# Attention with L1 distances on one core: where the key terms are added, and the order of three small VectorE instructions

## Chip, core and metric

The kernel runs on one core of a Trainium2 chip. The time is device microseconds of one execution. Before the change it is 8382.76 us, the median of 3 runs (8380.82 to 8383.2).

The engines are called as in the profile: PE is TensorE, with PEld for its weight loads, DVE is VectorE, ACT is ScalarE, SP is SyncE.

## What is computed

A tokenizer, an attention block and a feed-forward block with experts, for 8 batches of 750 tokens with 64 channels, in float32. The change touches the attention alone:

```python
scale = 1.0 / sqrt(q.shape[-1])                       # width 64
a = -sum(abs(q[:, s] - k[:, t]), axis=-1) * scale     # for every query s and key t, 8 heads
a = concatenate([a, zeros((b, 1, t, h))], axis=1)     # one more logit, zero
a = softmax(a, axis=1)[:, :t]                         # over the queries
bf = einsum('bsdh,bshw->bdhw', a, vf)
bb = einsum('bdsh,bshw->bdhw', a, vb)
```

The kernel uses |q - k| / 2 = max(q, k) - (q + k) / 2. The maxima are made on DVE, the absolute values on ACT, and what belongs to q alone or k alone is added apart: per query in the bank `kept`, per key in `kx`. The softmax is exp, divided by one plus its sum.

## The kernel before

`build` runs three phases: `phase_tokens`, `phase_attend`, `phase_feed`. `phase_attend` takes from about 300 to 8120 us of the span.

**Tiling.** It works through NPAIR = 16 pairs (8 batches, two groups g of four heads), in a hardware loop over the batches with both groups written out. A pair has NT = 24 tiles. The 128 partitions of a tile are 4 heads x 32 keys, its columns are the 750 queries, in two halves of 375. A tile has eight quads of keys (the last tile of a pair has four) and every quad two parts of 32 channels. The first quad has both parts merged into one row, so a full tile has 15 rows and the last one 7; a pair has STEPS = 352 rows.

**Rows and the ring.** A row is 128 x 3000 numbers in one of RING = 6 slots. Nearly half of the single rows (positions 1, 3, 5, 8, 10, 12, 14 of a tile) are made by ACT with Abs (L919), the others (2, 4, 6, 7, 9, 11, 13) by DVE with max and add (L1013). The merged row at position 0 is DVE's: four small instructions (L953) and a long one (L956), in `both`. PE sums each row over channels into the bank `sc` of the tile (L867, 16 matmuls of 375 columns a row). Each row waits for its slot (`ring_free`, counted up by PE), and PE for each row (`made_vec`, `made_act`).

**Order by hand.** Each engine's order is written out: constants at L759 say behind which row of a tile the other work of the tile before or after stands, and where a tile is shorter, behind its last row. Positions are those of the row list, and DVE itself makes no row at 8 and 10.

- EXP_AT = 6: ACT's `finish` takes exp of the finished bank of the tile before into `ex` (L903) and sums it into `zsum`; it counts up `ex_made`.
- FILL_AT = 8: DVE's `fill` (L943) sets the bank of the tile to come to `kept` plus the key term of that tile, one number a partition, `kx[:, g, t:t+1]`. It counts up `bank_set`, for which PE waits at the tile's start. In the last tile of a pair `key_sums` (L936) stands ahead of it, which takes the next pair's key terms out of PSUM, times -0.5.
- Z_AT = 8, RZ_AT = 9, A_AT = 10: DVE's `add_one` (L962), `invert` (L967) and `scale` (L972): one plus the sum, its inverse, and `ex` times the inverse. Each waits for the one before through a semaphore (`z_made`, `rz_made`, `a_made`). They stand in the order fill, plus one, row 9, inverse, scale, row 11.
- EXT_AT = 12: DVE's `turn` transposes the scaled tile (L985).
- On PE `back` (L815) behind row 2 and `forward` behind row 5 (L829) multiply the scaled tile with the values. `forward` is left out in every sixth tile; else it has 32 matmuls (the first of five) or 40.
- `sums` on PE (L841, L845), at the start of a pair's last tile, makes the query and key sums of the next pair in `kept`.

SP loads the next pair; no load is touched by the change.

Of the kernel before, what the change touches and what calls it, by code (L numbers as in the profile page):

```python
# [6 lines left out]
ALU = mybir.AluOpType  # L7
ACT = mybir.ActivationFunctionType
# [5 lines left out]
HALF = L // 2  # L14
# [54 lines left out]
def merged(t):  # L69

    return True
# [13 lines left out]
def first_step(t):  # L85

    return sum(len(steps(u)) for u in range(t))
# [635 lines left out]
def phase_attend(nc, sbuf, psum, semaphore, at, oacc, window, ratio, select, scratch_x, scratch_qk, scratch_ks, scratch_v):  # L723

    with ExitStack() as ctx:
# [30 lines left out]
        NV = STEPS - NA  # L756
        NM = sum(merged(t) for t in range(NT))
        KX = 400
        EXP_AT, FILL_AT, Z_AT, RZ_AT, A_AT, EXT_AT, KEEP_AT = 6, 8, 8, 9, 10, 12, 14  # L759
        BACK_AT, FORWARD_AT = 2, 5  # L760

        def rows(t):
# [7 lines left out]
        def due(place, i, t):  # L770

            return i == min(place, rows(t) - 1)
# [5 lines left out]
        with nc.Block() as block:  # L778
# [27 lines left out]
            def _(pe):  # L806
# [44 lines left out]
                def tile(n, g, t, b):  # L851

                    T = n * NT + t
                    bank = sc[t % 2]
                    pe.wait_ge(bank_set, T + 1)
                    if t == NT - 1:
                        pe.wait_ge(bank_set, (n + 1) * NT)
                        sums(1 - g, b + g)
                    for i, (quad, part) in enumerate(steps(t)):
                        if scalar_step(quad, part):  # L860
                            pe.wait_ge(made_act, n * NA + made_before(t, i + 1, True))
                        else:
                            pe.wait_ge(made_vec, n * NV + made_before(t, i + 1, False))
                        slot = (first_step(t) + i) % RING
                        for h in range(2):
                            for j in range(HALF_NH):
                                mm = pe.matmul(bank[32 * j:32 * j + 32, h, 0:HALF],  # L867
                                               window[:, min(part, 1), HALF_NH * g + j, QUADS - 1 - quad:QUADS + 31 - quad],
                                               ring[:, slot, j, h * HALF:(h + 1) * HALF],
                                               start=False, stop=(i == rows(t) - 1), skip_group_check=True)  # L870
                        mm.then_inc(ring_free, 1 if t < NT - 1 or i < rows(t) - 1 else 1 + TURN - STEPS)
                        if i == BACK_AT:
                            if t >= 2:
                                back(T - 2, g, t - 2, b)
                            else:
                                back(T - 2, 1 - g, NT - 2 + t, b)
                        if i == FORWARD_AT and t % GROUP:
                            if t >= GROUP:
                                forward(n * NT + (t // GROUP * GROUP - 1), g, t // GROUP - 1, t % GROUP - 1, GROUP - 1)
                            else:  # L880
                                forward(n * NT - 1, 1 - g, NG - 1, t % GROUP - 1, GROUP - 1)
# [15 lines left out]
            @block.scalar  # L897
            def _(act):

                def finish(par, done):  # L900

                    act.wait_ge(ring_free, done)
                    act.activation(ex[par][:, :].rearrange("p (h c) -> p h c", h=2)[:, :, 0:HALF], sc[par][:, :, 0:HALF],  # L903
                                   ACT.Exp, scale=-2.0 / D ** 0.5,
                                   accum_out=zsum[:, par:par + 1]).then_inc(ex_made, 1)

                def pair(b, g):

                    n = b * 2 + g
                    act.wait_ge(pair_in[g], b * (16 * NLOADS) + 16 * NLOADS)  # L910
                    act.mul(xs[g][:, 1, :, :], xs[g][:, 0, :, :], -0.5).then_inc(halves_made, 1)
                    act.wait_ge(halves_made, n + 1)
                    for t in range(NT):
                        for i, (quad, part) in enumerate(steps(t)):
                            k = first_step(t) + i
                            c = QUADS * t + quad
                            if scalar_step(quad, part):
                                act.wait_ge(ring_free, n * TURN + (k + 1))
                                act.activation(flat(ring[:, k % RING, :, :]), flat(qx[g][:, part, :, :]), ACT.Abs,  # L919
                                               bias=xs[g][:, 1, part, c:c + 1], scale=0.5).then_inc(made_act, 1)  # L920
                            if due(EXP_AT, i, t):
                                finish((t + 1) % 2, n * TURN + (first_step(t) + RING))

                with act.Fori(0, B) as b:
                    pair(b, 0)
                    pair(b, 1)
                act.wait_ge(ring_free, NPAIR * TURN + RING)
                finish((NT - 1) % 2, NPAIR * TURN + RING)

            @block.vector  # L930
            def _(vec):

                def key_sums(pairs, g):

                    vec.wait_ge(sums_made, pairs)
                    vec.tensor_scalar(kx[:, g, :], kept[:, 0, KX:KX + NT], -0.5, None, ALU.mult).then_inc(kx_made, 1)  # L936

                def fill(pairs, g, t):

                    par = t % 2  # L940
                    vec.wait_ge(kx_made, pairs)
                    if merged(t):
                        vec.tensor_scalar(sc[par][:, :, 0:HALF], kept[:, :, 0:HALF], kx[:, g, t:t + 1], None,  # L943
                                          ALU.add).then_inc(bank_set, 1)
                    else:
                        vec.tensor_copy(sc[par][:, :, 0:HALF], kept[:, :, 0:HALF]).then_inc(bank_set, 1)

                def both(n, g, t):

# [9 lines left out]
                def add_one(T, par):  # L959

                    vec.wait_ge(ex_made, T + 3)
                    vec.tensor_scalar(rz[:, par:par + 1], zsum[:, par:par + 1], 1.0, None, ALU.add).then_inc(z_made, 1)  # L962
# [34 lines left out]
                def pair(b, g):  # L997

                    n = b * 2 + g
                    vec.wait_ge(pair_in[g], b * (16 * NLOADS) + 16 * NLOADS)  # L1000
                    vec.wait_ge(halves_made, n + 1)
                    for t in range(NT):
                        T = n * NT + (t - 1)
                        par = (t + 1) % 2
                        for i, (quad, part) in enumerate(steps(t)):
                            k = first_step(t) + i
                            c = QUADS * t + quad
                            if not scalar_step(quad, part):
                                vec.wait_ge(ring_free, n * TURN + (k + 1))
                            if part == 2:  # L1010
                                both(n, g, t)
                            elif not scalar_step(quad, part):
                                vec.tensor_scalar(flat(ring[:, k % RING, :, :]), flat(qx[g][:, part, :, :]),  # L1013
                                                  xs[g][:, 0, part, c:c + 1], xs[g][:, 1, part, c:c + 1],
                                                  ALU.max, ALU.add).then_inc(made_vec, 1)
                            if due(FILL_AT, i, t):
                                vec.wait_ge(ex_made, n * NT + (t + 2))
                                if t == NT - 1:
                                    key_sums(n + 2, 1 - g)
                                    fill(n + 2, 1 - g, 0)  # L1020
                                else:
                                    fill(n + 1, g, t + 1)
                            if due(Z_AT, i, t):
                                add_one(T, par)
                            if due(RZ_AT, i, t):
                                invert(T, par)
                            if due(A_AT, i, t):
                                scale(T, par)
                            if due(EXT_AT, i, t):
                                if t:  # L1030
                                    turn(T, n, g, t - 1)
                                else:
                                    turn(T, n, 1 - g, NT - 1)
                            if t == GROUP and due(KEEP_AT, i, t):
                                keep(n, 1 - g, b + g)

                key_sums(1, 0)
                fill(1, 0, 0)
                with vec.Fori(0, B) as b:
                    pair(b, 0)  # L1040
                    pair(b, 1)
# [553 lines left out]
```

## Time and profile before

| | |
|---|---|
| median of 3 runs | 8382.76 us |
| the profiled execution | 8385.55 us |
| its span, first to last instruction | 8383.8 us |
| mean granted clock of PE | 0.989 |
| busy over the whole span | PE 8146.3 us (97%), DVE 7988.7 (95%), ACT 7685.1 (92%) |
| rows with Abs (L919) | 2624 of 2789 ns |
| matmuls of the rows (L867) | 90112, busy 7329.8 us |
| rows with max and add (L1013) | 2624 of 1832 ns |
| fill (L943) | 385 of 1002 ns |
| exp (L903) | 385 of 772 ns, and 189 ns each for reading the sum |

A view of the waits gives the time in total, how often, and the longest. A timeline row gives start, length, engine, line, operation and tiles; consecutive like instructions are merged into one row with their count, and brackets tell idle time before it and what ended it. Lengths of neighbours may overlap a little, so what an instruction costs its engine is read from start to start.

### The profile page before, as it was taken

What the parts mean: (1) busy time and instruction counts of PE and PEld (TensorE: products, weight loads), DVE (VectorE), ACT (ScalarE), POOL (GpSimd) and SP (SyncE); (2) the same over time, 40 slices, a digit from 0 to 9 for tenths busy, and PEclk for the clock granted to TensorE, in tenths of its full rate; (3) what the DMA queues carried; (4) which work ended last, traced back from release to release, by engine and by line L of the source; (5) the groups of instructions that cost most, each with busy time, mean ns of one, the idle gap of its engine ahead of it and who ended that gap; (6) DMA issues with size and microseconds to landing.
All of it is one profiled execution on the core that took longest, in us unless ns stands there. A gap on an engine that the chain in (4) does not pass through costs nothing. (4 is left out here: it accounts for less than half of the span.)

```text
span 8383.8 us, 244371 instructions
## 1 busy us (share of the span) xinstructions
PE 8146.3 (97%) x108456; PEld 3446.9 (41%) x108456; DVE 7988.7 (95%) x6906; ACT 7685.1 (92%) x3712; POOL 39.7 (0%) x36
## 2 busy tenths in 40 slices
PE   8699999999999999999999999999999999999999
PEld 3244444444444444444444444444444444444443
DVE  4699999999999999999999999999999999999984
ACT  3599999999999999999999999999999999999986
POOL 1000000000000000000000000000000000000000
PEclk9899999999999999999999999999999999999999
DMA  4310101001010100101010010101001010100000
GB/s 130 102 25 2 25 2 25 2 2 25 2 25 2 25 2 2 25 2 25 2 25 2 2 25 2 25 2 25 2 3 24 2 25 2 25 2 2 2 20 8
DMA packets 150392, 142.53 MB, mean 17 GB/s; under 512 B 115384, under 2 KB 121528, under 8 KB 148776
## 3 DMA queue, kind: packets, MB, share of 16 engines
q1 hardware_dynamic: 135711, 105.19, 5.4%
q10 hardware_dynamic: 13584, 21.06, 0.9%
q8 instruction: 891, 14.60, 0.7%
q14 instruction: 206, 1.69, 0.1%
HBM read 84.15 MB, written 42.05 MB: 15 GB/s over the span
## 5 line engine op out<-in xcount | busy, mean ns | idle before, releaser
L919 ACT ACTIVATE ring<-qx,xs 128x3000 f32<-128x3000 f32 x2624 | 7168.6, 2789 | 358.1 <-PE sc L867 357.5
L867 PE MATMUL sc<-ring,window 128*32 128x375 f32 x90112 | 7329.8, 479 | 118.9 <-DVE ring L956 114.8
L1013 DVE TENSOR_SCALAR ring<-qx,xs 128x3000 f32<-128x3000 f32 x2624 | 4711.7, 1832 | 1.5 <-PE sc L867 1.3
L867 PEld LDWEIGHTS sc<-ring,window 128*32 128x32 f32 x90112 | 2895.8, 109 | 4278.9 <-issue 3709.6
L956 DVE SCALAR_TENSOR_TENSOR ring<-qx,xs,ring 128x3000 f32<-128x3000 f32 x384 | 1284.1, 3344 | 13.5
L953 DVE TENSOR_SCALAR ring<-qx,xs,ratio 128x750 f32<-128x750 f32 x1536 | 925.5, 668 | 21.1 <-issue 15.7
L943 DVE TENSOR_SCALAR sc<-kept,kx 128x750 f32<-128x750 f32 x385 | 385.8, 1002 | 0.6
L985 DVE STREAM_TRANSPOSE exts<-ex 128x768 f32<-128x768 f32 x385 | 374.5, 973 | 0.6
L829 PEld LDWEIGHTS acc<-exts,vf 128*32 128x32 f32 x12480 | 283.0, 109 | 119.9 <-issue 118.7
L815 PE MATMUL acc<-ex,vb 128*32 128x376 f32 x3088 | 314.3, 478 | 1.5 <-DVE ex L972 1.5
L829 PE MATMUL acc<-exts,vf 128*32 128x96 f32 (+1 forms) x12480 | 310.6, 244 | 0.2 <-DVE exts L985 0.2
L903 ACT ACTIVATE ex<-sc 128x750 f32<-128x750 f32 x385 | 297.3, 772 | 6.7 <-PE sc L867 6.7
L972 DVE TENSOR_SCALAR ex<-ex,rz 128x768 f32<-128x768 f32 x385 | 239.1, 621 | 13.7
L815 PEld LDWEIGHTS acc<-ex,vb 128*32 128x32 f32 x3088 | 99.8, 108 | 145.0 <-issue 142.9
L1477 DVE SCALAR_TENSOR_TENSOR part<-pd,b2c,cb 128x500 f32<-128x500 f32 x48 | 35.5, 739 | 110.0 <-PE pd L1260 99.6
L641 ACT ACTIVATE qx<-pq,bqw,wkr 128x750 f32<-128x750 f32 x32 | 31.2, 975 | 117.8 <-issue 59.3
L1343 ACT ACTIVATE hid<-pu,b1c 128x1000 f32<-128x1000 f32 x96 | 99.8, 1088 | 39.9 <-PE pu L1240 39.8
L1240 PE MATMUL pu<-xt_d,w1t 64*128 64x500 f32 x384 | 96.7, 623 | 0.0
L710 DVE TENSOR_TENSOR exts<-pv,bv 120x1024 f32<-120x1024 f32 x34 | 40.2, 1220 | 54.2 <-PE pv L552 53.4
L1260 PE MATMUL pd<-hid,w2t 128*64 128x500 f32 x384 | 91.1, 595 | 0.6 <-DVE part L1477 0.6
L541 PE MATMUL pq<-oacc,w 64*128 64x375 f32 x128 | 32.1, 578 | 55.7 <-ACT qx L641 54.8
L552 PE MATMUL pv<-w,oacc 64*120 64x512 f32 x200 | 60.6, 727 | 13.6 <-DVE qx L710 13.6
(170 smaller groups left out, 915.8 us busy)
## 6 DMA issues: line engine op xcount, KB each, us to landing
qx<-scratch_qk SPq DMA_DIRECT2D x240, 187.5 KB
scratch_v<-exts SPq DMA_DIRECT2D x17, 960.0 KB, 7.8
scratch_qk<-qx ACTq DMA_DIRECT2D x32, 375.0 KB, 6.3
vb<-scratch_v SPq DMA_DIRECT2D x240, 46.0 KB
vf<-scratch_v SPq DMA_DIRECT2D x120, 88.0 KB
scratch_v<-qx SPq DMA_DIRECT2D x4, 960.0 KB, 6.6
scratch_v<-qx ACTq DMA_DIRECT2D x4, 960.0 KB, 8.9
qx<-scratch_qk ACTq DMA_DIRECT2D x16, 187.5 KB
```

The costliest lines, as they stand in the source:

```text
L815: pe.matmul(acc[g][32 * u:32 * u + 32, 0:COLS], vb[g][:, t, w0:w0 + 32], ex[t % 2][:, h * HPAD:h * HPAD + COLS], start=(t == 0), stop=Fals ...
L829: mm = pe.matmul(acc[g][32 * u:32 * u + 32, 0:COLS].rearrange("p (a c) -> p a c", a=2)[:, :, lo:lo + cols], vf[g][:, k, w0:w0 + 32], buf[: ...
L867: mm = pe.matmul(bank[32 * j:32 * j + 32, h, 0:HALF], window[:, min(part, 1), HALF_NH * g + j, QUADS - 1 - quad:QUADS + 31 - quad], ring[: ...
L903: act.activation(ex[par][:, :].rearrange("p (h c) -> p h c", h=2)[:, :, 0:HALF], sc[par][:, :, 0:HALF], ACT.Exp, scale=-2.0 / D ** 0.5, ac ...
L919: act.activation(flat(ring[:, k % RING, :, :]), flat(qx[g][:, part, :, :]), ACT.Abs, bias=xs[g][:, 1, part, c:c + 1], scale=0.5).then_inc( ...
L943: vec.tensor_scalar(sc[par][:, :, 0:HALF], kept[:, :, 0:HALF], kx[:, g, t:t + 1], None, ALU.add).then_inc(bank_set, 1)
L953: vec.tensor_scalar(ring[:, slot, j, :], qx[g][:, 0, j, :], xs[g][:, 0, 0, c:c + 1], ratio[:, HALF_NH * g + j:HALF_NH * g + j + 1], ALU.ma ...
L956: vec.scalar_tensor_tensor(flat(ring[:, slot, :, :]), flat(qx[g][:, 1, :, :]), xs[g][:, 0, 1, c:c + 1], flat(ring[:, slot, :, :]), ALU.max ...
L972: vec.tensor_scalar(ex[par][:, :], ex[par][:, :], rz[:, par:par + 1], None, ALU.mult).then_inc(a_made, 1)
L985: vec.transpose(ext[(NG * g + t // GROUP) % 2][:, :, :, t % GROUP, :], ex[t % 2][:, :]).then_inc(ext_made, 1)
L1013: vec.tensor_scalar(flat(ring[:, k % RING, :, :]), flat(qx[g][:, part, :, :]), xs[g][:, 0, part, c:c + 1], xs[g][:, 1, part, c:c + 1], ALU ...
L1343: act.activation(hid[n % 2][:, u, :, :], pu[u][:, :, 0:EC], ACT.Relu, bias=b1c[:, 2 * e + u:2 * e + u + 1]).then_inc(relu_made, 1)
```

## The change

- Key terms are no longer added when the bank is filled. `fill` copies `kept` alone, and `finish` gives the key term to exp as its bias, from `kx[:, g, t:t+1]` of the tile that it finishes. As exp is taken of -0.25 times the bank, `key_sums` scales by 1/8 instead of -0.5.
- In the first tile of a pair ACT waits for `kx_made` ahead of exp, PE waits for it ahead of `sums`, `fill` waits for `sums_made` instead of `kx_made`, and a memset of `kx[:, 1, :]` stands once ahead of all.
- `add_one` stands ahead of `fill` instead of behind it, and `invert` right behind `fill` (RZ_AT 8 instead of 9), with row 9 between it and `scale`.

```diff
-        EXP_AT, FILL_AT, Z_AT, RZ_AT, A_AT, EXT_AT, KEEP_AT = 6, 8, 8, 9, 10, 12, 14
+        EXP_AT, FILL_AT, Z_AT, RZ_AT, A_AT, EXT_AT, KEEP_AT = 6, 8, 8, 8, 10, 12, 14
...
                     if t == NT - 1:
                         pe.wait_ge(bank_set, (n + 1) * NT)
+                        pe.wait_ge(kx_made, n + 2)
                         sums(1 - g, b + g)
...
-                def finish(par, done):
-
+                def finish(g, t, done):
+
+                    par = t % 2
                     act.wait_ge(ring_free, done)
                     act.activation(ex[par][:, :].rearrange("p (h c) -> p h c", h=2)[:, :, 0:HALF], sc[par][:, :, 0:HALF],
-                                   ACT.Exp, scale=-2.0 / D ** 0.5,
+                                   ACT.Exp, scale=-2.0 / D ** 0.5, bias=kx[:, g, t:t + 1],
                                    accum_out=zsum[:, par:par + 1]).then_inc(ex_made, 1)
...
                             if due(EXP_AT, i, t):
-                                finish((t + 1) % 2, n * TURN + (first_step(t) + RING))
+                                if t == 0:
+                                    act.wait_ge(kx_made, n + 2)
+                                if t:
+                                    finish(g, t - 1, n * TURN + (first_step(t) + RING))
+                                else:
+                                    finish(1 - g, NT - 1, n * TURN + RING)
...
                     vec.wait_ge(sums_made, pairs)
-                    vec.tensor_scalar(kx[:, g, :], kept[:, 0, KX:KX + NT], -0.5, None, ALU.mult).then_inc(kx_made, 1)
-
-                def fill(pairs, g, t):
+                    vec.tensor_scalar(kx[:, g, :], kept[:, 0, KX:KX + NT], 1.0 / D ** 0.5, None, ALU.mult).then_inc(kx_made, 1)
+
+                def fill(pairs, t):
 
                     par = t % 2
-                    vec.wait_ge(kx_made, pairs)
-                    if merged(t):
-                        vec.tensor_scalar(sc[par][:, :, 0:HALF], kept[:, :, 0:HALF], kx[:, g, t:t + 1], None,
-                                          ALU.add).then_inc(bank_set, 1)
-                    else:
-                        vec.tensor_copy(sc[par][:, :, 0:HALF], kept[:, :, 0:HALF]).then_inc(bank_set, 1)
+                    vec.wait_ge(sums_made, pairs)
+                    vec.tensor_copy(sc[par][:, :, 0:HALF], kept[:, :, 0:HALF]).then_inc(bank_set, 1)
...
+                            if due(Z_AT, i, t):
+                                add_one(T, par)
                             if due(FILL_AT, i, t):
                                 vec.wait_ge(ex_made, n * NT + (t + 2))
                                 if t == NT - 1:
                                     key_sums(n + 2, 1 - g)
-                                    fill(n + 2, 1 - g, 0)
+                                    fill(n + 2, 0)
                                 else:
-                                    fill(n + 1, g, t + 1)
-                            if due(Z_AT, i, t):
-                                add_one(T, par)
+                                    fill(n + 1, t + 1)
                             if due(RZ_AT, i, t):
                                 invert(T, par)
...
+                vec.memset(kx[:, 1, :], 0.0).then_inc(kx_made, 1)
                 key_sums(1, 0)
-                fill(1, 0, 0)
+                fill(1, 0)
```

## Rows read from the trace of the kernel before

**Rows 1.** Busy time by window: us of window, PE, PEld, DVE, ACT, POOL, PEclk, DMA, GB/s.

```profile
1000.00:8000.00 7000.00, 6896.27 (x94876) 2927.42 (x94872) 6952.21 (x5821) 6678.40 (x3062) 0.00 (x0) 1.00 0.05 11
```

**Rows 2.** Waits from 1000 to 8000 us: total us, times, longest.

```profile
ACT ring L919 <- PE sc L867: 321.0, 677, 6.2
...
PE sc L867 <- DVE ring L956: 100.0, 60, 5.6
...
DVE ring L953 <- PE sc L867: 4.7, 9, 0.6
```

**Rows 3.** Timeline of DVE, two tiles from fill to fill, and the next L956.

```profile
7972.63 1.00 DVE L943 TENSOR_SCALAR sc<-kept,kx 128x750 f32<-128x750 f32 x1
7973.54 0.15 DVE L962 TENSOR_SCALAR rz<-zsum 128x1 f32<-128x1 f32 x1
7973.60 1.84 DVE L1013 TENSOR_SCALAR ring<-qx,xs 128x3000 f32<-128x3000 f32 x1
7975.35 0.16 DVE L967 RECIPROCAL rz<-rz 128x1 f32<-128x1 f32 x1
7975.55 0.62 DVE L972 TENSOR_SCALAR ex<-ex,rz 128x768 f32<-128x768 f32 x1
...
7980.45 2.41 DVE L953 TENSOR_SCALAR ring<-qx,xs,ratio 128x750 f32<-128x750 f32 x4
...
7993.16 1.00 DVE L943 TENSOR_SCALAR sc<-kept,kx 128x750 f32<-128x750 f32 x1
...
8023.95 3.34 DVE L956 SCALAR_TENSOR_TENSOR ring<-qx,xs,ring 128x3000 f32<-128x3000 f32 x1
```

**Rows 4.** Timeline of PE in the same stretch, to the end of a bare tile.

```profile
7974.00 1.01 PE L829 MATMUL acc<-exts,vf 128*32 128x96 f32 x40
7974.82 15.46 PE L867 MATMUL sc<-ring,window 128*32 128x375 f32 x192
7990.10 0.81 PE L815 MATMUL acc<-ex,vb 128*32 128x376 f32 x8
...
8011.26 15.34 PE L867 MATMUL sc<-ring,window 128*32 128x375 f32 x192
8027.35 3.05 PE L867 MATMUL sc<-ring,window 128*32 128x375 f32 x36 [0.75 <-DVE ring L956]
```

**Rows 5.** Groups of DVE instructions by form: busy us, mean ns, idle before.

```profile
L943 DVE TENSOR_SCALAR sc<-kept,kx 128x750 f32<-128x750 f32 x385 | 385.8, 1002 | 0.6
L972 DVE TENSOR_SCALAR ex<-ex,rz 128x768 f32<-128x768 f32 x385 | 239.1, 621 | 13.7
L363 DVE TENSOR_SCALAR state<-ps 128x750 f32<-128x750 f32 x24 | 22.6, 940 | 38.2 <-PE ps L296 38.2
L993 DVE COPY oacc<-acc 128x375 f32 x8 | 4.3, 544 | 0.0
```

**Rows 6.** Timeline of a pair's end, DVE and then PE.

```profile
3721.32 0.18 DVE L936 TENSOR_SCALAR kx<-kept 128x24 f32<-128x24 f32 x1
3721.54 1.01 DVE L943 TENSOR_SCALAR sc<-kept,kx 128x750 f32<-128x750 f32 x1
3722.45 0.15 DVE L962 TENSOR_SCALAR rz<-zsum 128x1 f32<-128x1 f32 x1
3722.64 0.16 DVE L967 RECIPROCAL rz<-rz 128x1 f32<-128x1 f32 x1
3722.84 0.62 DVE L972 TENSOR_SCALAR ex<-ex,rz 128x768 f32<-128x768 f32 x1
...
3730.20 4.00 PE L867 MATMUL sc<-ring,window 128*32 128x375 f32 x48 [3.08 <-DVE ring L956]
```

**Rows 7.** Groups of ACT instructions by form.

```profile
L903 ACT ACTIVATE ex<-sc 128x750 f32<-128x750 f32 x385 | 297.3, 772 | 6.7 <-PE sc L867 6.7
L1343 ACT ACTIVATE hid<-pu,b1c 128x1000 f32<-128x1000 f32 x96 | 99.8, 1088 | 39.9 <-PE pu L1240 39.8
```

**Rows 8.** The table load of ACT at L911, same view.

```profile
L911 ACT ACT_TABLE_LOAD x8 | 10.3, 1283 | 7.8 <-PEq L469 7.7
```

More of the change, by code:

```diff
@@ L927, in _ @@
                 act.wait_ge(ring_free, NPAIR * TURN + RING)
-                finish((NT - 1) % 2, NPAIR * TURN + RING)
+                finish(1, NT - 1, NPAIR * TURN + RING)
             @block.vector
```

## The prediction

> **What bounds the kernel now.** I read the views in this order: the page's busy times and slices, the busy time of the long middle window, the list of waits, then single instructions of two or three tiles on each engine, then a pair's end.
>
> The middle window holds the attention stage, at full granted clock. TensorE (PE), VectorE (DVE) and ScalarE (ACT) are all over 95% busy in it [rows 1], so shares don't name the bound and the waits have to. In the same 7000 us DVE's line L953 waited 4.7 us for PE, in nine places. PE waited 100 us for DVE's line L956, in 60 places, and ACT waited 321 us for PE [rows 2]. The chain is ACT behind PE and PE behind DVE, with DVE behind nobody: DVE's own instructions, start to start, are the period. The page's chain view doesn't help, since it covers 3% of the span, in the last stage.
>
> One tile, from fill to fill on DVE, is 7993.16 - 7972.63 = 20.53 us [rows 3]. PE does a tile's work in less. A run of matmuls has a recorded tail that overlaps the next work: 7974.82 + 15.46 - 7990.10 = 0.18 us. Twelve steps that run on without a wait are recorded as 15.34 us, less the tail 15.16 us, or 1.263 us a step; twelve around a tile's start, where PE meets line L956, take 7990.10 - 7974.82 = 15.28 us [rows 4]. So PE loses 0.12 us at the start of a tile with 40 matmuls of `forward`. A tile without `forward` (every sixth) leaves 0.75 us of recorded idle time, 0.93 us with the tail [rows 4]. A tile with 32 of them (also every sixth) is shorter than one with 40 by 8 x 0.82 / 40 = 0.16 us, and loses 0.28 us. PE's own work is therefore 20.41 us in a 40-tile, 20.25 in a 32-tile, 19.60 in a bare one. A pair has 23 full tiles: 15, 4 and 4 of these, a mean of 20.24 us. That is the floor once DVE is faster than PE: 0.29 us a tile below today.
>
> ACT is busy 95.4% of the window [rows 1], or 19.6 us of 20.53.
>
> **The change, part by part.**
>
> *Fill without a pointer operand (L943, 385 times).* It is 1002 ns for 750 columns, from PSUM to PSUM, with one operand read from a [128,1] tile [rows 5]. The nearest rows without such an operand are 940 ns for 750 columns from PSUM to SBUF (L363) and 544 ns for a COPY of 375 columns from PSUM (L993) [rows 5]. The two differ by 396 ns for 375 columns, that is 1.05 ns a column, so the copy isn't in a double-rate mode. With 1.04 ns a column the fixed parts are 221 ns (L943), 159 (L363) and 154 (L993). L972, SBUF to SBUF at half that per column, has 621 - 400 = 221 with one pointer, while L962 is 0.15 us for one column with an immediate [rows 3, 5]. Two pairs of rows thus give 62 to 70 ns for the pointer and almost nothing for PSUM against SBUF as the target. I take 65 ns. Bounds: 0 (if writing PSUM and not the pointer costs it) and 72.
>
> *The order of the three small instructions.* Now: fill, plus one, a ring row, inverse, scale. L967 starts at 7975.35 and L972, which waits for its result, at 7975.55 [rows 3]: 0.20 us for an instruction of 0.16 us; at the pair's end L962 and L967, each waited for in the same way, show 0.19 and 0.20 [rows 6]. I take 0.195. Where nothing depends on the instruction ahead, the next starts 0.09 us before that one's recorded end: L962 to L1013 is 0.06 us [rows 3]. At a pair's end, where `z_made` has to be waited for at once, the same L967 starts 0.19 us after L962 [rows 6], and between ring rows L967 starts before the row's end [rows 3]. The cost is that of the pair, not of the line. In the new order plus one stands ahead of the fill (0.85 us cover `z_made`), the inverse behind it, and a ring row (1.75 us) between inverse and scale covers `rz_made`. The inverse then costs 0.07 instead of 0.195: 0.125 us a tile. If the cover were gone it would be today's cost. Bounds 0 and 0.135.
>
> By the Trainium skill ("VectorE: DVE Perf Modes", section "The DRAIN you can't avoid") eight copies with a semaphore after each took as long as eight with one at the end, so a semaphore between neighbours would cost nothing, and this term would be nil. The rows here speak against it, with 0.195 beside 0.06 us; it is a rival below.
>
> *A full tile:* 0.065 + 0.125 = 0.19 us, all on the path, as DVE waits for nobody. 23 x 16 = 368 tiles: 69.9 us.
>
> *A pair's end (16 times).* Key terms, fill, plus one, inverse, scale stand together. From L936 to L972 it is 3722.84 - 3721.32 = 1.52 us [rows 6]. Of this 0.22 us is the step from L936 to the fill, which waits for `kx_made`. After: plus one 0.06, key terms 0.09 (0.18 less the 0.09 overlap, since the copy needs no key term), fill 0.91 - 0.065 = 0.845, inverse and its wait 0.195: 1.19 us. It saves 0.33 us, and PE sits idle 3.08 us just behind it [rows 6], so all of it counts: 5.3 us.
>
> *Exp with a bias.* It is 772 ns for 750 columns now [rows 7]; at 0.833 ns a column its fixed part is 147. L1343 (bias read from a tile) has 1088 - 833 = 255 [rows 7]. So the operand costs some 108 ns, and I add 0.11 us a tile to ACT. ACT has 0.93 us a tile free, 0.74 after the shorter period and 0.63 with the bias: nothing, and nothing either at twice the price. Its results have room: in the middle window no wait of DVE for ACT is listed, and DVE reaches the fill (and then plus one, behind the same wait) no sooner than now but for the 0.19 us. Only the very last exp stands bare: +0.1 us once.
>
> *Waits.* Plus one now waits for `ex_made` ahead of the fill, which waited for the same value before: nothing new. ACT's `kx_made` wait at a pair's first exp and PE's ahead of `sums` ask for a value set at the previous pair's end, many us earlier. Behind ACT's would stand ring rows, behind PE's a whole tile. The memset lies in DVE's wait for the first `sums`. No DMA or queue is moved.
>
> *What is late next.* DVE's new period is 20.34 us. PE in a 40-tile needs 20.41, so PE falls 0.07 behind in each of four tiles in a row, 0.28 in all, and regains it in the bare tile. DVE may only run ahead by what the ring of six slots allows. It begins the merged row (L953) at 7980.45, for which PE must have finished step 9: 7974.82 + 4 x 1.263 + tail 0.18 = 7980.05, and 0.06 for the release (as L956's end at 8027.29 to PE's start at 8027.35) [rows 3, 4]. Room is 0.34 us, 0.15 after a saving of 0.19, less the lag at the tile's start (0, 0.07, 0.14, 0.21). So DVE is held up by some 0.06 us once in six tiles: 0.06 x 3 x 16, about 3 us.
>
> **Sum.** 69.9 + 5.3 - 0.1 - 3 = 72 us. The profiled execution took 8385.55 us with a span of 8383.8, 2.8 us above the median. I carry the saving to the median: 8382.76 - 72 is 8311 us.
>
> **Rivals.**
>
> *PE takes over in the 40-tiles.* If the ring's room is really nil, lag can't be carried and 15 tiles a pair run at 20.41 instead of 20.34: 15 x 16 x 0.07 = 17 us lost of 75, 8325 us. For: the room is small, and PE's ends are modelled. Against: DVE waited for PE in so few places.
>
> *The copy costs as much as the sum.* Writing PSUM from PSUM has no row without a pointer. Then 0.125 x 368 + 0.265 x 16 = 50 us are gained, less held-up time: 8334 us.
>
> *Waiting costs nothing.* What looks like a wait would belong to the scale itself: it starts late behind whatever stands ahead. Then only the copy saves, 0.065 x 384 = 25 us: 8358 us. Against: L967 appears with both spacings [rows 3, 6]. The skill's DRAIN section, above, would give this time.
>
> *ACT becomes last (slower).* Place: exp, between ring rows 5 and 8 of ACT. If exp with its bias needs another table than the Abs rows around it, two loads a tile come in. ACT would have 19.6 + 2 x 1.28 = 22.2 us a tile: 1.6 x 384 = 620 us more, 9000 us. It decides from 0.93 us of extra work a tile. The 1.28 us is that of the loads in this trace, which has one at L911 in half of the pairs [rows 8] and none between Abs and Exp; a bias doesn't change the function, so it is unlikely.
>
> *More than forecast.* If the overlap is deeper than 0.09 us, the saving goes on until PE's floor: 0.29 x 368 + 5 = 112 us, 8271 us; half of the way from the forecast is 8291.
>
> *It does nothing.* The gaps close elsewhere on DVE (each moved instruction takes up the saving as another stall): within 0.2%.
>
> **How the numbers follow.** The forecast has 0.62; PE takes over 0.13; costly copy 0.10; waiting costs nothing 0.04; more than forecast 0.05; nothing 0.03; slower 0.03. The range goes from 8297 (with the upper bounds of both terms, 0.207 us a tile, and nothing held up, 82 us are gained, 8301, and 4 us are for scatter and for a start of the case of more) to 8336 (costly copy with 2 us of scatter). What lies outside (waiting costs nothing, most of more than forecast, nothing, slower) is some 0.15. A measurement of this kernel tells about 0.2%, 17 us, from no change: all cases but the last two are faster by more, so faster 0.94, same 0.03, slower 0.03.
>
> **What the profile will show.** Fill a COPY of 930 to 940 ns; L967's successor 0.07 us behind it and the scale without idle time ahead; 20.34 us from fill to fill; exp 870 ns, with ACT's wait for PE down by a quarter or more; PE's recorded idle time at bare tiles down from 0.75 to some 0.3; 2.4 to 2.8 us instead of 3.08 at a pair's end; a few more waits of L953 for PE. The prediction is wrong if the copy stays at 1000 ns, if the scale still stands 0.03 us or more behind its predecessor, or if L953 waits for PE in most tiles.

## The result and the profile after

The changed kernel takes 8318.88 us (median of 4 runs, 8315.86 to 8326.73), beside 8382.98 us for the kernel before (4 runs): a ratio of 0.9923, 95% interval 0.9911 to 0.9936, or 64 us less. The forecast was 72 us less, 8311 us, in a range of 8297 to 8336. A second series of the changed kernel (5 runs, below) has 8323.09 us beside 8385.2, 62 us less. The profiled execution of after took 8326.73 us, its slowest, with a span of 8324.7.

The groups of the page of after (busy us, mean ns, idle before), to be held against [rows 5, 7]; the rows of L921 and L868 are those of L919 and L867 in the table of before:

```profile
L921 ACT ACTIVATE ring<-qx,xs 128x3000 f32<-128x3000 f32 x2624 | 7162.0, 2790 | 265.3 <-PE sc L868 261.5
L868 PE MATMUL sc<-ring,window 128*32 128x375 f32 x90112 | 7311.4, 479 | 86.8 <-DVE ring L959 86.6
...
L949 DVE COPY sc<-kept 128x750 f32<-128x750 f32 x385 | 359.9, 935 | 0.0
...
L905 ACT ACTIVATE ex<-sc,kx 128x750 f32<-128x750 f32 x385 | 333.5, 866 | 6.6 <-PE sc L868 6.6
...
L975 DVE TENSOR_SCALAR ex<-ex,rz 128x768 f32<-128x768 f32 x385 | 236.0, 613 | 0.6
```

The fill is 935 ns for 1002, the exp 866 for 772, and the idle time ahead of the scale is 0.6 us in all instead of 13.7. A tile on DVE, from plus one to plus one (timeline: start, length, both us):

```profile
3602.82 0.14 DVE L965 TENSOR_SCALAR rz<-zsum 128x1 f32<-128x1 f32 x1
3602.88 0.93 DVE L949 COPY sc<-kept 128x750 f32<-128x750 f32 x1
3603.73 0.15 DVE L970 RECIPROCAL rz<-rz 128x1 f32<-128x1 f32 x1
3603.80 1.82 DVE L1016 TENSOR_SCALAR ring<-qx,xs 128x3000 f32<-128x3000 f32 x1
3605.54 0.61 DVE L975 TENSOR_SCALAR ex<-ex,rz 128x768 f32<-128x768 f32 x1
...
3623.14 0.15 DVE L965 TENSOR_SCALAR rz<-zsum 128x1 f32<-128x1 f32 x1
```

The inverse now costs 3603.80 - 3603.73 = 0.07 us from start to start, and the scale begins before the ring row ahead of it has ended (3603.80 + 1.82 = 3605.62). The tile is 20.32 us, 20.33 in most, where it was 20.53. The end of a pair, DVE and then PE, answers to [rows 6]:

```profile
3702.79 0.15 DVE L965 TENSOR_SCALAR rz<-zsum 128x1 f32<-128x1 f32 x1
3702.86 0.17 DVE L943 TENSOR_SCALAR kx<-kept 128x24 f32<-128x24 f32 x1
3702.95 0.94 DVE L949 COPY sc<-kept 128x750 f32<-128x750 f32 x1
3703.79 0.15 DVE L970 RECIPROCAL rz<-rz 128x1 f32<-128x1 f32 x1
3703.98 0.62 DVE L975 TENSOR_SCALAR ex<-ex,rz 128x768 f32<-128x768 f32 x1
...
3711.34 1.14 PE L868 MATMUL sc<-ring,window 128*32 128x375 f32 x9 [2.43 <-DVE ring L959]
```

It takes 3703.98 - 3702.79 = 1.19 us for 1.52, and PE idles 2.43 us instead of 3.08. The waits from 1000 to 8000 us, as [rows 2]:

```profile
ACT ring L921 <- PE sc L868: 236.7, 389, 6.0
...
PE sc L868 <- DVE ring L959: 74.3, 64, 5.0
...
DVE ring L956 <- PE sc L868: 11.3, 11, 2.2
...
DVE ring L1016 <- PE sc L868: 5.1, 16, 0.7
```

ACT waits a quarter less for PE and PE a quarter less for DVE, while DVE has begun to wait for PE now and then. That is where a part of the gain went. From the start of the first L956 or L959 to that of the last, the attention stage, it is 7796.5 us before and 7729.5 after: 67.0 us saved. The terms, each summed over all tiles from the starts of that line:

| | forecast, us | measured, us |
|---|---|---|
| shorter period of 368 full tiles | 69.9 | 73.6 (0.20 each) |
| ends of pairs | 5.3 | 4.7 (in 15 of 16) |
| DVE held up in the long tiles | -3 | -6 |
| first tile behind the loop's turn and the start | 0 | -4.3 |
| sum | 72 | 68 |

Rounding the period to 0.01 us is the last 1 us. The profiled executions differ by 58.8 us and not by 67.0 because attention began at 309.5 us in the trace of before and at 318.0 in that of after; in a second trace of after it began at 306.6, and the earlier phases are the same code in all. Such scatter outside the stage may also be what separates 67 us from the 64 of the medians; no trace shows it for these.

### The profile page after: what moved, and what is told of

Same layout as the page of the kernel before. It is cut to its first block and busy times, and to the rows that moved or that the text cites. A ratio compares the mean times of both kernels' runs of the same rounds, so it can differ in the third digit from the quotient of the medians.

```text
span 8324.7 us, 244412 instructions
## 1 busy us (share of the span) xinstructions
PE 8114.0 (97%) x108456; PEld 3999.8 (48%) x108456; DVE 7931.1 (95%) x6907; ACT 7711.0 (93%) x3712; POOL 39.7 (0%) x36
## 5 line engine op out<-in xcount | busy, mean ns | idle before, releaser
L921 ACT ACTIVATE ring<-qx,xs 128x3000 f32<-128x3000 f32 x2624 | 7162.0, 2790 | 265.3 <-PE sc L868 261.5
L868 PE MATMUL sc<-ring,window 128*32 128x375 f32 x90112 | 7311.4, 479 | 86.8 <-DVE ring L959 86.6
L868 PEld LDWEIGHTS sc<-ring,window 128*32 128x32 f32 x90112 | 3424.7, 110 | 3689.3 <-issue 2751.4
L1016 DVE TENSOR_SCALAR ring<-qx,xs 128x3000 f32<-128x3000 f32 x2624 | 4705.7, 1829 | 5.3 <-PE sc L868 5.1
L959 DVE SCALAR_TENSOR_TENSOR ring<-qx,xs,ring 128x3000 f32<-128x3000 f32 x384 | 1283.9, 3343 | 13.6
L956 DVE TENSOR_SCALAR ring<-qx,xs,ratio 128x750 f32<-128x750 f32 x1536 | 924.8, 665 | 22.1 <-PE sc L868 11.9
L949 DVE COPY sc<-kept 128x750 f32<-128x750 f32 x385 | 359.9, 935 | 0.0
L905 ACT ACTIVATE ex<-sc,kx 128x750 f32<-128x750 f32 x385 | 333.5, 866 | 6.6 <-PE sc L868 6.6
```

What stands on the lines that cost most here:

```text
L868: mm = pe.matmul(bank[32 * j:32 * j + 32, h, 0:HALF], window[:, min(part, 1), HALF_NH * g + j, QUADS - 1 - quad:QUADS + 31 - quad], ring[: ...
L956: vec.tensor_scalar(ring[:, slot, j, :], qx[g][:, 0, j, :], xs[g][:, 0, 0, c:c + 1], ratio[:, HALF_NH * g + j:HALF_NH * g + j + 1], ALU.ma ...
L959: vec.scalar_tensor_tensor(flat(ring[:, slot, :, :]), flat(qx[g][:, 1, :, :]), xs[g][:, 0, 1, c:c + 1], flat(ring[:, slot, :, :]), ALU.max ...
```

## Experiments

The order, copy, immediate and spread kernels ran beside 10 runs of the kernel before with a median of 8386.25 us, the bias, ring and loop-turn kernels beside 15 runs with 8384.91, the last two beside 9 with 8385.2.

**The order alone.** The kernel before, with `RZ_AT` 8 and `add_one` ahead of `fill`:

```diff
-        EXP_AT, FILL_AT, Z_AT, RZ_AT, A_AT, EXT_AT, KEEP_AT = 6, 8, 8, 9, 10, 12, 14
+        EXP_AT, FILL_AT, Z_AT, RZ_AT, A_AT, EXT_AT, KEEP_AT = 6, 8, 8, 8, 10, 12, 14
...
+                            if due(Z_AT, i, t):
+                                add_one(T, par)
                             if due(FILL_AT, i, t):
```

> The kernel before with the new order alone: plus one ahead of the fill, inverse right behind it, the key term still added in the fill. Theory (the wait for a neighbour's result costs DVE 0.125 us): from fill to fill 20.53 becomes 20.40 to 20.41 us, the idle time ahead of the scale (13.7 us in all before) is gone, and the time falls by 0.125 x 368 + 0.13 x 16 = 48 us, to 8333 to 8338. Rival (the scale starts late by itself, waiting costs nothing): scale still 0.03 us behind its predecessor's end, 20.50 us or more, less than 10 us gained. At 20.41 us DVE is as slow as PE in its longest tiles, so no tile should be held up by the ring.

Measured: 8336.34 us (4 runs), ratio 0.9942, interval 0.9927 to 0.9958, 50 us less. From the DVE timeline:

```profile
3515.75 1.00 DVE L943 TENSOR_SCALAR sc<-kept,kx 128x750 f32<-128x750 f32 x1
3516.66 0.15 DVE L967 RECIPROCAL rz<-rz 128x1 f32<-128x1 f32 x1
3516.73 1.83 DVE L1013 TENSOR_SCALAR ring<-qx,xs 128x3000 f32<-128x3000 f32 x1
3518.47 0.62 DVE L972 TENSOR_SCALAR ex<-ex,rz 128x768 f32<-128x768 f32 x1
```

The inverse costs 0.07 us, and the scale starts before the ring row ahead of it has ended (3516.73 + 1.83 = 3518.56). The period is 20.39 us in every full tile but 0 and 6 (6 has `keep`, 0.45 us more in all kernels), so the order is worth 0.14 us a tile, a little over the forecast's 0.125. The rival that waiting costs nothing is out.

**The copy alone.** The kernel after, in the old order (fill, plus one, row, inverse, scale; the reverse of the diff above):

> The kernel after with the old order: fill as a copy, then plus one, a ring row, inverse, scale; key terms as the bias of exp. Theory (the pointer operand costs 0.065 us): 20.46 us from fill to fill, 0.065 x 368 plus 16 pair ends of 0.19 us, 27 us gained, 8353 to 8358. Rival (the gain of the change is mostly in the copy, the order is worth nothing): 20.33 us, 8320. The gains of this kernel and of the one with the order alone should add up to more than that of the change, by what the ring takes back (7 us by the trace of after).

Measured: 8358.52 us (5 runs), ratio 0.9968, interval 0.9955 to 0.9981, 28 us less; the period is 20.47 us. The inverse and the scale stand 0.20 us apart again:

```profile
3512.79 0.16 DVE L970 RECIPROCAL rz<-rz 128x1 f32<-128x1 f32 x1
3512.99 0.62 DVE L975 TENSOR_SCALAR ex<-ex,rz 128x768 f32<-128x768 f32 x1
```

The two gains are 50 and 28 us, 78 together; the change itself has 62 to 64 at its medians. In the traces the attention stage is 26.2 us shorter with the copy, 47.5 with the order and 67.0 with both (68.9 in the second trace of after), so 5 to 7 us are missing in the sum, as expected; the rest of what is missing in the medians is within their scatter. The copy alone leaves DVE above the 20.41 us that PE needs in a long tile, and the order alone brings it to 20.39, where no tile is held up yet. Both together bring it 0.08 us below.

**Operand or operation.** The kernel after with

```diff
-                    vec.tensor_copy(sc[par][:, :, 0:HALF], kept[:, :, 0:HALF]).then_inc(bank_set, 1)
+                    vec.tensor_scalar(sc[par][:, :, 0:HALF], kept[:, :, 0:HALF], 0.0, None, ALU.add).then_inc(bank_set, 1)
```

> The kernel after with the fill as an addition of the immediate 0.0 instead of a copy, PSUM to PSUM as before. If the operand read from a tile cost the time, the fill takes 935 to 945 ns and a tile 20.33 to 20.34 us, 8316 to 8321 in all. If it was the addition as against a copy, it takes 1000 ns, a tile 20.39 us, and 24 us of the gain are gone (8340).

Measured: 8317.59 us (4 runs), ratio 0.9919, interval 0.9903 to 0.9934. Its group:

```profile
L949 DVE TENSOR_SCALAR sc<-kept 128x750 f32<-128x750 f32 x385 | 361.0, 938 | 0.0
```

938 ns, as the copy. What cost 64 ns in L943 is the operand that is read from a tile, not the addition and not PSUM as the target.

**Exp with a bias alone.** The kernel before, with a tile of zeros:

```diff
-                                   ACT.Exp, scale=-2.0 / D ** 0.5,
+                                   ACT.Exp, scale=-2.0 / D ** 0.5, bias=kz[:, par:par + 1],
```

> The kernel before with exp given a bias read from a tile of zeros; all else as before. Theory (ACT has 0.9 us a tile to spare): exp 865 to 870 ns instead of 772, ACT's wait for PE 30 to 40 us less, a tile still 20.53 us, the time within 4 us of before. Rival (ACT's lateness reaches PE or DVE): each tile longer by up to 0.1 us, 35 us slower.

Measured: 8384.03 us (10 runs) beside 8384.91 (15 runs), ratio 0.9999, interval 0.999 to 1.0008. The group of exp, and ACT's wait from 1000 to 8000 us:

```profile
L905 ACT ACTIVATE ex<-sc,kz 128x750 f32<-128x750 f32 x385 | 333.4, 866 | 6.6 <-PE sc L869 6.6
```

```profile
ACT ring L921 <- PE sc L869: 271.1, 472, 6.0
```

ACT is busy 31 us more in these 7000 us (6709.87 for 6678.40), which is 94 ns for each of some 336 tiles. It comes out of ACT's wait for PE, 271 us for 321, and no tile is longer (20.53). ACT pays for the operand in time it has.

**Is it the ring that takes gain back?** In after, DVE's periods are 20.33 us, tiles 0 and 6 apart, but for the tiles 10, 11, 16, 17 and 22 of a pair, with means of 20.39, 20.44, 20.38, 20.43 and 20.40. They are the last tiles with 40 matmuls of `forward` before a bare one or the pair's end. Here is tile 11 of one pair, DVE and PE, and one row of the bare tile behind it:

```profile
3588.30 1.80 DVE L1016 TENSOR_SCALAR ring<-qx,xs 128x3000 f32<-128x3000 f32 x1
3590.09 2.42 DVE L956 TENSOR_SCALAR ring<-qx,xs,ratio 128x750 f32<-128x750 f32 x4
...
3608.72 1.80 DVE L1016 TENSOR_SCALAR ring<-qx,xs 128x3000 f32<-128x3000 f32 x1
3610.43 2.41 DVE L956 TENSOR_SCALAR ring<-qx,xs,ratio 128x750 f32<-128x750 f32 x4
...
3583.96 1.02 PE L829 MATMUL acc<-exts,vf 128*32 128x96 f32 x40
3584.79 15.37 PE L868 MATMUL sc<-ring,window 128*32 128x375 f32 x192
...
3616.27 4.00 PE L868 MATMUL sc<-ring,window 128*32 128x375 f32 x48 [0.31 <-DVE ring L959]
```

PE's row 9 ends at 3584.79 + 4 x 1.263 + 0.18 = 3590.02 us, and with 0.06 for the release DVE may start at 3590.08; it starts at 3590.09, 1.79 us behind the start of the row ahead where a tile later it is 1.71. PE's idle time at the bare tile is 0.31 us for 0.75: PE was behind and caught up there. Two experiments press on this from both sides.

*Less room:* `RING = 5`.

> The kernel after with five slots in the ring instead of six. Theory (DVE begins the merged row of the next tile only when PE has finished the row six before it, with some 0.15 us to spare): with five slots it has to wait for one row more, 1.26 us. From the end of row 10 on PE, the release and the tail take 0.24 us, the merged row 2.45 + 3.26 us and its release 0.06 us, in which PE has only four rows (5.05 us) to do: it stands still 1.0 us a tile. A tile takes 21.2 us in the mean, all 8620 to 8670 us. L956 waits for PE in nearly every tile. Rival (the ring has room to spare and the small hold-ups of tiles 10, 11, 16, 17, 22 come from elsewhere): 8315 to 8330 us.

Measured: 8681.17 us in one run, beside 8384.91 us. PE and DVE timelines:

```profile
3502.36 4.00 PE L868 MATMUL sc<-ring,window 128*32 128x375 f32 x48 [0.98 <-DVE ring L959]
...
3511.25 11.56 PE L868 MATMUL sc<-ring,window 128*32 128x375 f32 x144
3523.67 4.00 PE L868 MATMUL sc<-ring,window 128*32 128x375 f32 x48 [0.85 <-DVE ring L959]
...
3517.82 2.41 DVE L956 TENSOR_SCALAR ring<-qx,xs,ratio 128x750 f32<-128x750 f32 x4 [0.60 <-PE sc L868]
```

Row 10 ends at 3511.25 + 5 x 1.263 + 0.18 = 3517.75, released 0.06 later: L956 starts at 3517.82. PE stands still 0.85 us as recorded, 1.03 with the tail. The place is as expected; the total is 11 us above the range given. Most long tiles came to 21.48 us, 32-tiles to 21.31, bare ones to 20.65, the mean of all full tiles to 21.4 us, where 21.2 was expected. L956 waits for PE 313 times between 1000 and 8000 us, in nearly every tile, but the single rows (L1016) wait too, 271 times and 99 us in all, which the expectation didn't have. This single run is far outside of what the rival gave.

*Shorter tiles:* the forward products of a pair's first two groups in six parts of 32 matmuls instead of four of 40 and one of 32, so that the tiles 7 to 18 are alike:

```diff
-                        if i == FORWARD_AT and t % GROUP:
-                            if t >= GROUP:
-                                forward(n * NT + (t // GROUP * GROUP - 1), g, t // GROUP - 1, t % GROUP - 1, GROUP - 1)
+                        if i == FORWARD_AT and t and t != GROUP:
+                            q = (t - 1) // GROUP
+                            parts = GROUP if q in (1, 2) else GROUP - 1
+                            if q:
+                                forward(n * NT + (q * GROUP - 1), g, q - 1, (t - 1) % GROUP, parts)
                             else:
-                                forward(n * NT - 1, 1 - g, NG - 1, t % GROUP - 1, GROUP - 1)
+                                forward(n * NT - 1, 1 - g, NG - 1, t - 1, parts)
```

> The kernel after with the forward products of a pair's first two groups of tiles cut into six parts (32 matmuls each) instead of five, so that tiles 7 to 18 need 20.25 us of PE each and none needs 20.41. Theory (PE's lag in its long tiles uses up the room in the ring and holds DVE up): tiles 10, 11, 16 and 17, at 20.36 to 20.46 us in the trace of after, come to 20.33; tile 22 keeps its 20.40; PE's recorded idle time in the bare tiles is gone. 0.35 x 16 = 5 to 6 us faster than after. Rival (those tiles are slow for another reason, such as a port or the clock): they keep 20.40 to 20.45, and the time stays within 2 us.

Measured: 8313.46 us (5 runs), ratio 0.9915, interval 0.9901 to 0.9928. The tiles 10, 11, 16 and 17 are at 20.33 us in the mean of all pairs, tile 22 keeps 20.38. Summed over the tiles 1 to 22, 5.3 us less than in after are above the common period. PE's timeline at a bare tile that has become a 32-tile:

```profile
3587.38 3.97 PE L868 MATMUL sc<-ring,window 128*32 128x375 f32 x48
3591.17 0.84 PE L829 MATMUL acc<-exts,vf 128*32 128x96 f32 x32
3591.83 15.44 PE L868 MATMUL sc<-ring,window 128*32 128x375 f32 x192
3607.08 0.81 PE L815 MATMUL acc<-ex,vb 128*32 128x376 f32 x8
```

From 3591.17 to the same row 20.33 us later nothing is idle by more than the 0.09 us that the twelve rows' 15.25 us have over 15.16. The comparison was repeated with both kernels side by side:

> The changed kernel once more, beside the one with six forward parts, to compare the two on one chip. 8313 to 8322 us; tiles 10, 11, 16, 17 and 22 at 20.35 to 20.45 us as in its first trace; at the loop's turns tile 0 is held up by the PE time lost to the clock less 0.5 to 1.0 us.

> Six forward parts in the first two groups of a pair, as before. Theory (ring room): 4 to 7 us less than the changed kernel beside it. Rival (the gain in the tiles is given back elsewhere): within 2 us of it.

Measured: 8323.09 us (8314.81 to 8323.8, 5 runs) for the changed kernel and 8313.62 us (8312.33 to 8320.47, 5 runs) for the other. The medians differ by 9.5 us, more than expected, but the ranges overlap: the ratios to before are 0.9925 (0.9912 to 0.9939) and 0.9916 (0.9902 to 0.9929). What the traces carry is 5 us in the held-up tiles: the tiles 1 to 22 are 5.8 us above the common period in the changed kernel and 0.7 in the other. The whole attention stage is only 2.7 us shorter in this pair of traces (7725.0 for 7727.7), since the first tiles behind the loop's turn, below, are held up by 2.7 us more; in the pair before it was 4.3 us shorter (7725.2 for 7729.5). So it is shown that the held-up tiles go back to the common period when no tile needs 20.41 us of PE. That the whole kernel is faster by it isn't clear of the noise, though both medians of this kernel are the lowest of all that were tried.

**Behind the loop's turn.** The first tile of a pair behind the turn of the hardware loop is longer in both kernels. In after, in one such place (PE timeline, then granted clock in windows, the third number from the right):

```profile
1288.61 6.71 PE L868 MATMUL sc<-ring,window 128*32 128x375 f32 x45 [4.78 <-DVE ring L959]
```

```profile
1288.00:1292.00 4.00, 3.39 (x21) 1.26 (x25) 4.00 (x3) 2.22 (x3) 0.00 (x0) 0.50 0.01 4
...
1296.00:1300.00 4.00, 4.00 (x56) 1.80 (x52) 3.63 (x6) 3.64 (x2) 0.00 (x0) 1.00 0.00 0
```

PE was idle for 4.78 us, then ran at half the full clock, the 1.2 GHz level, and 45 matmuls took 6.71 us where 48 take 4.00. It falls behind, and DVE is held up once the ring's room is used. With the PE time lost to the clock behind each of the seven turns, from windows of 1 us, and the hold-up of the tile there:

| kernel | period, us | lost to clock, seven turns, us | hold-up, us | at a loss near 3.0 | at a loss near 1.5 |
|---|---|---|---|---|---|
| before | 20.53 | 14.3 | 5.8 | 1.77 | 0.15 to 0.18 |
| copy alone | 20.47 | 12.8 | 5.7 | 1.85 | 0.26 to 0.70 |
| order alone | 20.39 | 16.0 | 9.5 | 2.22 | 0.47 |
| after | 20.33 | 17.3 | 11.8 | 2.09, 2.55 | 0.71, 0.78 |
| after, second trace | 20.33 | 14.1 | 8.7 | 2.11 | 0.58 to 0.84 |

At about the same loss the hold-up is 0.3 to 0.8 us larger after than before. The difference of the two sums, a seventh of it for each turn, is what the ring's room takes up: 1.21 us before, 1.01 with the copy, 0.93 with the order, 0.79 and 0.77 after. It shrinks with DVE's period, and 1.21 - 0.79 is 3 us in seven turns that are due to the change. The rest of the difference is that the loss itself differs from turn to turn (1.4 to 3.1 us) and from trace to trace; why it does stays open. The first tiles of the other pairs are held up by 3.0 us in all before and 1.3 after, so that the term of the table above is 4.3 us in this trace of after and 2.0 in the second. An attempt to keep PE busy there:

```diff
+                    if t == 0 and g == 0:
+                        for _ in range(36):
+                            pe.matmul(acc[1][:, 400:512], select[:, :], ksum[:, 0:112], start=True, stop=True,
+                                      skip_group_check=True)
                     pe.wait_ge(bank_set, T + 1)
```

These matmuls start sums of their own in the bank in which the sums of `acc[1]` stand. This kernel and the next don't compute the reference's output, presumably because they disturb those sums; that wasn't tested apart. The work and its order are otherwise those of after.

> The kernel after with 36 small matmuls (bf16, 112 columns, into columns of a bank that nobody reads) ahead of the first tile of every second pair, where the loop turns and PE is idle for 4.8 us; in the trace of after PE's granted clock falls to the half just there and PE's slow first rows hold DVE up for 0.7 to 2.5 us (13.1 us in all over the 20.33 us of a tile, 8.8 before the change). Theory (the idle time lets the clock fall): the clock stays at 1.00 behind the loop's turn, tile 0 takes 20.3 to 20.8 us there, 6 to 10 us are gained on after. Rival (the hold-up is of another kind, or the matmuls don't keep the clock up): tile 0 stays at 21 to 22.9 us, no gain, or up to 2 us lost where the small matmuls are in the way.

Measured: 8337.41 us (5 runs), ratio 0.9944, interval 0.993 to 0.9958, 14 to 19 us slower than after. PE's timeline and a window:

```profile
1274.98 0.26 PE L857 MATMUL acc<-ksum,select 128*128 128x112 bf16 x2 [2.35 <-issue]
1278.05 3.35 PE L857 MATMUL acc<-ksum,select 128*128 128x112 bf16 x34 [2.81 <-issue]
1281.33 5.08 PE L872 MATMUL sc<-ring,window 128*32 128x375 f32 x48
```

```profile
1276.00:1280.00 4.00, 1.95 (x22) 1.96 (x23) 4.00 (x3) 3.03 (x3) 0.00 (x0) 0.59 0.02 4
```

PE can't start them: it stands 2.35 us and, two matmuls on, 2.81 us more with no wait that the profile names. The first of these stops is in the trace of after too, at the branch that closes the loop on PE (L890; count, length in ns, start in us):

```profile
L890 PEldq COMPARE_BRANCH  x1: 3866/3866/3866, 1282.4 to 1282.4; - x1
L890 PEldq FUSED_REGOPS  x1: 63/63/63, 1286.3 to 1286.3; - x1
```

There PE is idle from 1283.83 to 1288.61 us and its branch ends at 1286.22. So 2.4 of the 4.8 us that the profile puts down to a wait for L959 are PE's own stop; for the other 2.4 PE waits for DVE, which had a stop of 2.2 us at its own branch. Whether a second stop of 2.8 us hides under that wait isn't shown. In the kernel with the small matmuls the clock has fallen by the time they run (0.59), they take 0.1 us each and the first tile is later still (23 to 25 us behind the turns), a loss well beyond the 2 us that the rival allowed. These matmuls don't hold the clock. Whether it would stay up if PE had no idle time there, and what would remove PE's stop, wasn't tried.

> The small matmuls at the loop's turn together with the forward products cut into six parts. If the two hold-ups are separate, both gains add up: 12 to 15 us on after, 8302 to 8307 us. If only the spread works, 8313 us.

Measured: 8328.19 us (5 runs), ratio 0.9933, interval 0.992 to 0.9947. That misses both figures given. As the small matmuls cost time instead of saving it, what is left is that this cost and the gain of the spread stand side by side: 9 us less than with the small matmuls alone.

## Why the prediction was right

**The bound.** DVE's own instructions from start to start were the period, in before and in all variants with six slots, but for the few tiles in which PE holds them up: 20.53, 20.47, 20.39 and 20.33 us follow from what was taken off DVE, and 94 ns more on ACT moved nothing.

**Fill.** Forecast 65 ns, bounds 0 and 72; measured 67 (1002 to 935), and 64 with the immediate. The pairs of rows in [rows 5] were the right neighbours.

**Order.** Forecast 0.125 us; measured 0.14 (20.53 to 20.39), just past the upper bound of 0.135. The Trainium skill's "VectorE: DVE Perf Modes", section "The DRAIN you can't avoid", by which a semaphore between two copies costs nothing extra, would have given about 0 here. In this trace and the order experiment, with their 0.14 us, it doesn't hold for an instruction whose operand the one right ahead has made.

**Ends of pairs.** Forecast 1.19 us where it was 1.52, measured 1.19.

**Exp.** Forecast 108 ns, measured 94. The Trainium skill's "ScalarE: Activation LUTs", section "What ACT_TABLE_LOAD costs", says that an operand read per partition adds about 93 ns; the trace agrees, with 94. No table load came in: L913 has eight as L911 had [rows 8].

**What was mis-sized.** Two terms, both under "what is late next". The hold-up in the long tiles was put at 3 us and is 6. In a long tile of before DVE starts the merged row 0.57 us behind PE's start of row 10 (7980.45 and 7974.82 + 4 x 1.263 in [rows 3, 4]); where PE holds it up, as in the rows of tile 11 above, some 0.26 are left. So the room was 0.31 us and not 0.34, and the saving of 0.20, not 0.19, leaves 0.11. In after the distance is 0.38, 0.30, 0.27 and 0.29 us in the tiles 8 to 11: with a lag of 0.08 us for each long tile the room is gone one tile sooner than in the sum, and not one but two tiles of a group of six are held up, by 0.06 and 0.11 us. Against that, the first group of a pair has next to none: there `forward` has 88 columns instead of 96 (0.79 us for 32 matmuls, not 0.84, in the trace of before), which fits. And the first tile behind the loop's turn wasn't in the sum at all, though the kernel before shows it (21.81 us in one place): a tile in which PE is slow eats room that DVE's earlier finish has used up. Without both the stage would have gained 78 us.

**Rivals.** "PE takes over in the 40-tiles" (8325 us) is the nearest to what happened, at a third of its price (6 us for 17). Costly copy, waiting costs nothing and a later ACT are ruled out by the runs above.

## What to carry to other kernels

Where an engine waits for nobody, read its instructions from start to start and look for neighbours of which one needs the other's result: a row of other work between them costs nothing and gave 0.14 us a tile here. A per-partition operand can be moved from the engine that bounds to one that waits, even if it costs more there (94 ns on ACT for 67 on DVE). Before summing such gains, subtract the next engine's work tile by tile, not in the mean: here its long tiles and its slow restart behind the loop's turn took 10 of 78 us back, and making the tiles alike returned 5 in the tiles, though not clearly in the whole time.

## What the runs showed of the hardware

- In the rows shown, an instruction of DVE that waits for the result of the one right ahead starts 0.04 us behind its end; the others start 0.08 to 0.10 us before the end of the one ahead.
- A PSUM to PSUM copy of 750 float32 columns takes 935 ns, an addition of an immediate 938, of an operand read from a tile 1002.
- At the turn of the hardware loop DVE stood still for 2.2 to 2.5 us and PE for 1.9 to 2.4 us with no wait that the profile names; with small matmuls put there PE stopped a second time, for 2.7 to 3.0 us. PE's stop stood under a wait for another engine in the list of waits until work was put there.
- Behind 4.8 us of idle time PE's granted clock was at the 1.2 GHz level (0.50 from 1288 to 1292 us) and at 1.00 from 1296 us on. In the kernel before, behind 5.6 us of idle time, it was 0.62 from 3240 to 3244 us and 1.00 from 3248 on.
